# A four-block graph network on one core: rows picked by TensorE matmuls are gathered by GpSimd instead

## The reference, cut to what matters

```python
msgs = x[src]                                             # SAGE, twice
agg = segment_sum(msgs, dst) / maximum(deg, 1.0)[:, None]
out = agg @ Wl + b + x @ Wr

alpha = sum(q[dst] * k[src], axis=-1) * SCALE             # attention, three times
a = exp(alpha - segment_max(alpha, dst)[dst]);  a = a / segment_sum(a, dst)[dst]
out = segment_sum(v[src] * a[:, :, None], dst)

agg = segment_max(h[src], dst)                            # GIN, twice
x = (h + agg) @ W + b
```

## Time and profile before

| | |
|---|---|
| median of three runs | 8466.71 us |
| lowest and highest | 8452.32 and 8481.12 us |
| span of the profiled execution | 8485.5 us |
| mean granted PE clock | about 0.76 of full |
| bytes moved by DMA | 1216 MB, mean 143 GB/s |

### The profile page before, as it was taken

The page is one execution under the profiler, slowest core; times in us unless marked ns, Lnnn a source line. Parts: engine busy times, 40 slices in busy tenths (PEclk is TensorE's granted clock), DMA queues, the critical chain, the costliest instruction groups (busy, mean ns, idle before and its releaser), DMA issues.

```text
span 8485.5 us, 85732 instructions
## 1 busy us (share of the span) xinstructions
PE 5156.1 (61%) x29027; PEld 3057.3 (36%) x29027; DVE 4943.7 (58%) x9372; ACT 2594.1 (31%) x6303; POOL 4930.4 (58%) x5102
## 2 busy tenths in 40 slices
PE   4766658888454554345555345455537887667777
PEld 2333334444333333233333223333313444334443
DVE  6666645555666666667676677767773333333333
ACT  2333312121344444345454434545430000000000
POOL 6666656665455656455565546556635555565555
PEclk8777778898776766667677667767758888778887
DMA  3444435554344444344444444444424454345453
GB/s 126 142 138 142 140 111 165 172 166 160 113 147 143 150 142 149 119 137 148 147 153 146 125 130 151 149 144 151 150 68 149 157 163 158 123 150 163 159 161 126
DMA packets 464201, 1216.31 MB, mean 143 GB/s; under 512 B 109489, under 2 KB 142271, under 8 KB 463752
## 3 DMA queue, kind: packets, MB, share of 16 engines
q1 hardware_dynamic: 263180, 721.75, 23.9%
q0 software_dynamic: 200576, 489.04, 20.9%
HBM read 736.73 MB, written 473.62 MB: 143 GB/s over the span
## 4 chain that ended last, share of the span: by engine, by line
PE 37%; issue 27%; another core or an unknown queue 13%; DVE 12%; ACT 7%; DMA 2%; DVEq 1%; POOL 1%; SPq 0%; POOLq 0%; ACTq 0%
PE banks_ps L1608 13%; PE banks_ps L1624 11%; PE cin_ps L1608 4%; PE cout_ps L1608 4%; PE pair_ps L1608 4%; ACT hot_small L1327 3%; DVE work L895 2%; DVE pair_ps L855 1%; ACT outs L1351 1%; DVE UA L857 1%; DVEq L849 1%; DVE pair_ps L850 1%; DMA hot_small<-kept_hots 1%; ACT work L1336 1%
## 5 line engine op out<-in xcount | busy, mean ns | idle before, releaser
L1961 POOL DMA_INDIRECT arena<-table,near_idx x4732 | 4584.2, 969 | 2872.3 <-issue 1399.6
L1608 PE MATMUL banks_ps<-arena,work 128*128 128x384 bf16 x6750 | 1371.2, 353 | 473.6 <-issue 386.5
L1608 PEld LDWEIGHTS banks_ps<-arena,work 128*128 128x128 fp8e4 (+1 forms) x6750 | 685.1, 103 | 1107.8 <-issue 761.0
L850 DVE COPY_PREDICATED pair_ps<-near_late,pair_ps 128x896 f32<-128x896 uint8 x336 | 368.3, 1096 | 1025.3 <-ACT pair_ps L1370 740.8
L1624 PE MATMUL banks_ps<-arena,hot_small 128*128 128x256 bf16 x2025 | 620.5, 306 | 321.3 <-issue 320.7
L1624 PE MATMUL banks_ps<-work,hot_small 128*128 128x256 bf16 x2025 | 621.2, 307 | 300.4 <-issue 300.2
L1624 PE MATMUL banks_ps<-arena,hot_both 128*128 128x256 bf16 x2025 | 612.9, 303 | 295.0 <-issue 294.8
L1624 PE MATMUL banks_ps<-work,hot_both 128*128 128x256 bf16 x2025 | 613.4, 303 | 284.3 <-issue 283.8
L895 DVE TENSOR_TENSOR_SCAN work<-work,banks_ps 128x1024 f32<-128x1024 f32 x336 | 768.1, 2286 | 11.5
L1298 ACT COPY near_idx<-src_i 128x7 int32<-128x7 int32 x784 | 151.1, 194 | 1983.4 <-DVE outs L758 1747.1
L786 DVE TENSOR_REDUCE arena<-banks_ps 128x128 f32<-128x384 f32 x324 | 179.7, 555 | 872.7 <-remote 725.9
(11 more groups left out here) (267 smaller groups left out, 8639.3 us busy)
## 6 DMA issues: line engine op xcount, KB each, us to landing
rows_plain<-outs SPq DMA_DIRECT2D x448, 448.0 KB
work<-kept_hots SPq DMA_DIRECT2D x432, 400.0 KB
rows_att<-outs SPq DMA_DIRECT2D x336, 504.0 KB
arena<-table,near_idx POOLq DMA_INDIRECT x4732
kept_hots<-hot_small SPq DMA_DIRECT2D x162, 400.0 KB
hot_small<-kept_hots SPq DMA_DIRECT2D x81, 400.0 KB
hot_both<-kept_hots SPq DMA_DIRECT2D x81, 400.0 KB
table<-arena SPq DMA_DIRECT2D x18, 512.0 KB, 3.0
```

The source lines that it names most:

```text
L850: chain(v.copy_predicated(prod, near_late[:, s, :].unsqueeze(2).to_broadcast(wide), next_q.unsqueeze(1).to_broadcast(wide)))
L1608: ins = pe.matmul(pick_bank[u], hot[:, t, :], parts3[:, :, t, :], start=(t == 0), stop=(t == NB - 1))
L1961: pool.indirect_dma_start(dst, None, tab, bass.IndirectOffsetOnAxis(ap=idx, axis=0))\
```

## The change

PE picks no rows any more, in any pass. `PICKS` and all that it needs go: one-hots, their tile numbers, their narrowing, store and loads, the three bf16 parts of the node tables, the laying of picked rows, and the semaphores of all of these. POOL gathers all 784 steps of each pass. The seven small matmuls of `count_degrees` stay. `bias_row`, which shared room with one-hots, has its own, and SP no longer waits for picks before it loads it. Two rows of the set-up (`first_i`, `tile_base`) go, so the counts that others wait for on `s_const` fall by one. Ring, groups, loops and the order of all that stays are the same. In the changed file the numbers of lines are other ones: L1961 is L1601 there.

```diff
-WIDE = [1, 0, 1, 0]
-PICKS = {0: [1, 1, 1, 1], 1: [2, 1, 2, 1], 2: WIDE, 3: WIDE, 4: WIDE, 5: [2, 1, 2, 1], 6: [2, 1, 2, 1]}
-KEPT = 6
...
-        hot_small = sb("hot_small", [P, NB * P], F8)
+        bias_row = sb("bias_row", [P, 4 * D])
...
-            each = 16 * (GROUP - picks(k, s))
-            return it * each + (16 * GROUP + land_base[k][s])
+            return it * (16 * GROUP) + (16 * GROUP + 16 * GROUP * LOOPS * k)
...
                 for j in range(GROUP):
-                    if picked and j == GROUP - 1 - len(picked):
-                        whole_rows(k, it, s)
                     prev = out_plain[:, s, j - 1, :] if j else out_plain[:, (s - 1) % RING, GROUP - 1, :]
                     ready(s_agg, first + (agg_base[k] + j))
                     row = ring_plain[:, s, j, :]
-                    for i, (u, step_of) in enumerate(picked):
-                        if j == step_of:
-                            v.wait_ge(s_whole, pick_number(k, it, s) + (i + 1))
...
-                    if ahead and j < PIECES:
-                        one_hot(k, ahead_it, ahead_s, j)
...
-                if picks(k, s) and not (isinstance(it, int) and it == 0):
-                    v.wait_ge(s_whole, pick_number(k, it, s) + 1)
                 chain(v.tensor_tensor(prod, prod, ring[:, s, :, 0:D], ALU.mult))
...
                     for s in range(RING):
-                        if s == 1:
-                            take_apart(k)
                         plain_group(k, 0, s)
...
                     projected(2, "qkvs2", b, 4)
-                    take_high(2, b)
...
-                elif stage == 7:
-                    take_middle(2, b)
...
                         stage_group(k, it + 1, s, far)
-                        lay_pick(k, it + 1, s)
...
-                        if made(k, s) and it + 1 < LOOPS:
-                            number_tiles(k, it + 1, s)
-
                         act.wait_ge(s_agg, it * (RING * GROUP) + (agg_base[k] + (s + 1) * GROUP))
                         if it + 1 < LOOPS:
                             stage_group(k, it + 1, s)
-                        ahead_it, ahead_s = two_on(it, s)
-                        if made(k, ahead_s) and ahead_it not in (0, LOOPS):
-                            narrow(k, ahead_it, ahead_s)
...
-            pick_rows(0)
+            for it in range(LOOPS):
+                for s in range(RING):
+                    count_degrees(it, s)
...
-            pick_wide(2)
             carry_turns(2)
...
                                      slot_out(k, s).rearrange("p j f -> p (j f)")).then_inc(s_store[s], 16)
-                        if k in hot_made:
-                            keep(k, *two_on(it, s))
-                        if KINDS[k] == ATT:
-                            for n, (on_it, on_s) in enumerate(wide_picks(k)):
-                                if n > 1 and max(on_it * RING + on_s - 7, 0) == g:
-                                    load_wide(k, n)
...
-            def rows_of_group(k, s, n=GROUP):
-                for j in range(n):
+            def rows_of_group(k, s):
+                for j in range(GROUP):
                     row = ring[:, s, j, :] if KINDS[k] == ATT else ring_plain[:, s, j, :]
                     fetch(row, table[k], near_idx[:, s, 0, j:j + 1], s_land[s])
...
                             staged(k, it, s)
-                            rows_of_group(k, s, GROUP - picks(k, s))
+                            rows_of_group(k, s)
```

303 lines of the change are left out of this document (19 added, 284 removed).

## The result

The changed kernel takes 8625.01 us (median of four, 8609.26 to 8628.18) against 8470.02 us (four, 8452.32 to 8481.12) for the kernel before: ratio 1.0181, 95% interval 1.0162 to 1.0200. It is **slower by 1.8%**; forecast was 8270 in a range of 7735 to 8430.

A forecast was written before the change was run, and what follows sets the result against it. Waits bound the kernel, with engines obstructed during POOL's unbroken gathers; POOL would become the bound. Terms -7 + 12 - 54 - 125.5 - 24 = -198.5 gave 8287 us profiled, 8270 median, range 7735 to 8430.

The forecast's parts named there:

- The clock of the plain passes: Passes 0, 1, 5, 6: POOL gathers 784 steps at 1.248 us, 978 us a pass, plus small allowances and tails.
- 10 us for pauses I don't see yet: Passes 5 and 6: allowance of 10 us each for unseen POOL pauses, bounds 0 and 71.
- some 40 us, bounds 0 and 80: Pass 0: obstruction from PE's counting matmuls holding DVE's hots, about 8 POOL pauses of 5.14 us.
- The attention passes: Passes 2, 3, 4: 1048 us of gathers plus a 5.14 us pause every 3.5 groups; 1231.5 us each with tail.
- PE's part before: Attention passes before the change: a wide pick needs 16.1 us unobstructed but takes 22.8, so 6.7 us are obstruction.
- Before the attention passes, -24: Ahead of passes 2, 3, 4: table-splitting subtractions leave DVE, saving 8 us each, bounds 0 and 17.
- Rival 3: Plain passes: DVE gets stuck at about 84 instructions, POOL pauses 7.6 us each time; 8530 us in all; 10%.
- Rival 1: All passes: obstruction goes with PE's bursts, ACT never gets stuck, attention passes 1078.5 us each; 7770 us in all; 20%.

The follow-up runs named there:

- e6_idle: Changed kernel plus idle work: three ACT copies a group in pass 3, six PE matmuls in 4, one POOL memset in 5, three in 6; 8666.47 us.
- e2_scans_again: Changed kernel with one DVE instruction a group in pass 5 and fourteen half scans in pass 6, on chip 12 (held); 8694.86 us.

## Why the prediction was wrong

**The clock of the plain passes, 784 x 1.248, with 40, 0, 10 and 10 us for stops.** This is the step that failed: the forecast let POOL gather back to back through a whole plain pass, since PE, the engine that got stuck there before, was gone. By the windows, forecast and measured, they came to 1028 and 1130.2, 1002 and 1109.6, 1000 and 1086.5, 1001 and 1086.3 us. That is 382 us too little, more than the whole miss of 340 us (8626.5 against 8287 for the profiled execution). Two things stood in its place.

*Passes 5 and 6*: POOL itself is held. It gathers at 1.25 us only until it is some 26 us ahead of 1.40 us each; 1070.5 us from first to last gather against 978, 92 us for which the forecast had "10 us for pauses I don't see yet, bounds 0 and 71". My rows showed stretches of at most 50 gathers, 50 x 0.15 = 8 us ahead: the kernel before never came to the limit, and I took the pace of a stretch for the pace of a pass.

*Passes 0 and 1*: POOL keeps its 1.25 us and is never more than 13.5 us ahead of 1.40 us a gather, so that limit isn't reached. It stops for indices, because DVE and PE are held: 138.3 us of long stops in pass 0, where I had "some 40 us, bounds 0 and 80", and 108.5 in pass 1, where I had none. In pass 0 the sight was right, PE sticking at its 63 to 70 counting matmuls and DVE's `hots` after it; the stops were mis-sized, 20 of 2 to 10.5 us instead of 8 of 5.14. How much of them is PE's and how much DVE's own was not tried.

**The attention passes**, 1231.5 forecast, 1206.7, 1204.9 and 1210.5 measured, within about 2%, 72 us less in all. The mechanism was right here, and two sizes were wrong and offset each other: ACT gets some 65 instructions between stops, five groups, and not 45 in 3.5 groups, and a series of stops comes to 6.1 to 6.6 us, not 5.14. With these (5 x 9.36 + 6.5) / 5 = 10.7 us a group, 1194 us for 112; 1187.0, 1185.9 and 1190.9 were measured from first to last gather. There were 26 to 28 stops of over 2 us a pass, 23 of them "remote", where about 32 were announced. The copies of `e6_idle` moved them as a count of ACT's would. That the time came so near was in part luck.

All 4 x 784 + 3 x 840 = 5656 gathers x 1.40 give 7918 us, and the seven passes take 7917 from first to last gather together. I don't take that for an explanation: passes 5 and 6 are 27 below the rate and pass 1 is 7 below, the others are 10 to 24 above it, and only passes 5 and 6 show the limit. Whether one cause makes POOL's 1.40 and the other engines' stops isn't shown.

**PE's part before.** The 16.1 us for a pick were read off matmuls at the lower clock, 0.215 us apart. Most pick matmuls of the attention passes stand 0.110 us apart, 8.3 us for 75, so of the 22.8 us a pick more was waiting than the 6.7 us I saw. The sum doesn't use it.

**Before the attention passes, -24**: this came. From the head gather to the next pass's first it took 92.6, 71.7 and 83.8 us instead of 100.5, 79.5 and 87.3, 19 us less. It was lost again after passes 5 and 6, 66.9 and 67.2 us instead of 55.0 and 54.7. PE isn't the reason, which the prediction's range allowed 50 us for: PE is busy for about 23 us in each of these four stretches, and the granted clock is 0.50 to 0.54 there before as after. Free they take 47 to 50 us with either kernel. Held they take 54 to 56 us where POOL did not end the pass at its limit (the kernel before, `e6_idle`, pass 6 of `e2_scans_again`), so these 24 us seem to go with the limit too; that wasn't tried by itself.

**Rival 3**, DVE as the one that gets stuck in plain passes, was right for pass 1: it put 101 us on it, and 108.5 us of stops are there, the first after 99 DVE instructions. It had pass 0 at 91, where PE is in it as well. For passes 5 and 6 it had the right sight and the wrong cause: DVE's scans are held, the first at the 140th instruction of pass 6 and not at the 84th, but POOL never stops, and with one DVE instruction a group the pass takes as long. It was given 10%.

**Rival 1, no obstruction**, exists, on chips 8 and 9. I gave it 7770 us and 20%; the kernel that differs from the changed one only by idle work took 7690. But it isn't the picks that bring the obstruction: without it the kernel before takes 6870, and the change is 12% slower (7690.7 to 6876.04), since a plain pass then takes 984 to 988 us and an attention pass 1049 to 1052, near the 978 and 1048 costed, where they had taken 790 to 905 and 983 to 986: the picks had been free. A condition that comes with the chip can't be assumed for one side of a comparison alone. This is the second step that failed: the rival gave 20% to a gain of 700 us that no pair of runs showed.

**What can't be told.** The Trainium skill (NOTIFIC — the notification-queue block, on overflow) has internal buffers of the profiler's records that hold producers up. That POOL's instructions, a memset too, were charged the same 1.40 us for seven groups fits such an account, and so does a count for each engine; that 8 or 10 POOL instructions a group came to 9.8 us on the average does not. Every execution here has such records, the free ones too, so no run separates it, and records alone don't make the condition. What makes a chip held or free stays open. That a gather's landing isn't the limit is seen: the last landing of a group comes 2.2 to 2.6 us after the start of its last gather, at the beginning of pass 5 and at its end.

## What to carry to other kernels

Take the pace of a long unbroken run from a long unbroken run: a stretch of 50 gathers at 1.25 us says nothing of 784, if a limit has room for 26 us. If engines get stuck by a count of their instructions, taking one away doesn't end it: ask for each of the others, the relieving engine too, what it will be held at. Before an engine is relieved of work that another one gets, ask whether it was on the path at all: here a pick saved 1.2 us at no cost on one chip, and a wide pick lost about 1 us on another, so the choice that was best held (picks in the plain passes only, 0.981 of before) was 2.7% slower free. When a trace shows waits with no releaser, look whether other executions of the same kernel have them, before building a sum on them.

## What was not expected of the hardware

- Two conditions of the same kernel, 23% apart (8461 and 6863 us, chips 12 and 8), with unobstructed matmuls 0.215 us apart, gathers 1.25 us apart and the same busy time of DVE and POOL in pass 2 in both. What tells them apart are waits, most of them without a releaser.
- Held: 1.40 us a gather in passes 5 and 6, whatever the bytes (64 or 128 columns), the partitions (64 or 128), seven DVE instructions a group or one, idle instructions of ACT or PE, or POOL's pauses, after an advance of 26 to 27 us (24 to 26 with PE's idle matmuls). With fourteen DVE instructions a group POOL stops before it gets there (1104 us). Pass 5 came to 1070.5 to 1073.8 us in eight executions of five kernels; the exception is `e6_idle` at 1093.8, whose added memsets are POOL's own.
- Held: other engines' instructions start in steps of about 0.70 us (scans 0.7, 1.4 and 2.1 apart), and POOL's stops come after a count of them: some 65 of ACT in the attention passes, with three more copies a group (64) as without.
- Granted clock 0.50 (1.2 GHz) in every pass in which PE is idle, where it had been 0.69 to 0.87 with picks. In pass 0, with seven small matmuls a group, there is no clock record, and its matmuls keep the pace of the lower level. The same pick matmul goes at 0.215 us at 0.50 and at 0.110 us at 1.00.
